# Attention with a router beside it: routing products placed singly and in the seams, division apart from its copy, buffers that run on across blocks

## What is computed

```python
x = layernorm(x + attention(x))            # x: 2 x 2048 x 256, 16 heads of 16
n = layer_norm(x, g1, be1); x = x + n + (n @ mix_w + mix_b)
res = x; n = layer_norm(x, g2, be2)
probs = softmax(n @ router_w); topw, topi = top_k(probs, 2)       # 8 experts
y = sum over the two chosen experts of topw * (silu(n @ w1[e] + b1[e]) @ w2[e] + b2[e])
out = layernorm(x + (res + y))
```

## Time and profile before

| | |
|---|---|
| median of three executions | 1675.38 us |
| the profiled execution | 1675.51 us |
| its span, first to last instruction | 1673.8 us |
| busy: PE, ACT, DVE, POOL | 1610.3, 1244.0, 536.7, 469.3 us |
| exponentials, 116.6 to 1106 | 955.7 us busy of 989 |
| one routed block | 124.17 us |
| mean granted TensorE clock | 0.988 |

### The profile page before, as it was taken

The page is one execution under the profiler, slowest core; times in us unless marked ns, Lnnn a source line. Parts: engine busy times, 40 slices in busy tenths (PEclk is TensorE's granted clock), DMA queues, the critical chain, the costliest instruction groups (busy, mean ns, idle before and its releaser), DMA issues.

```text
span 1673.8 us, 45794 instructions
## 1 busy us (share of the span) xinstructions
PE 1610.3 (96%) x17936; PEld 916.9 (55%) x17941; DVE 536.7 (32%) x1443; ACT 1244.0 (74%) x1869; POOL 469.3 (28%) x495
## 2 busy tenths in 40 slices
PE   7989999999999999999999999999999999999990
PEld 5543333433433433433433433358999999999990
DVE  4551125435435425525525535526210000000004
ACT  5659999999999999999999999963444444444441
POOL 4630011112102202202202212115455444444441
PEclk9999999999999999999999999999999999999995
DMA  5776310101103442301100101646668766666645
GB/s 166 205 155 90 64 40 15 48 26 34 50 24 69 89 81 52 100 28 31 50 28 30 51 26 34 241 143 169 182 175 225 198 185 166 186 186 186 176 119 207
DMA packets 108487, 181.18 MB, mean 108 GB/s; under 512 B 14121, under 2 KB 80361, under 8 KB 108137
## 3 DMA queue, kind: packets, MB, share of 16 engines
q1 hardware_dynamic: 95010, 160.88, 33.2%
q0 software_dynamic: 13296, 17.77, 5.6%
HBM read 134.07 MB, written 40.18 MB: 104 GB/s over the span
## 4 chain that ended last, share of the span: by engine, by line
PE 81%; ACT 4%; issue 4%; DVE 1%; DMA 1%; POOL 0%; POOLq 0%; ACTq 0%; DVEq 0%
PE at_s L1385 24%; PE at_po L1397 23%; PE at_s L1511 14%; PE at_s L1524 14%; ACT place L1300 4%; PE at_small L1413 4%; PE at_small L1406 1%; PE at_po L1500 1%; DMA rows_out<-place,at_v 1%; DVE cb_ln_stats L696 1%; DVE place L1750 0%; POOL place L1254 0%; DMA place<-rows_out 0%; POOL place L1259 0%; DVE at_v L1714 0%
## 5 line engine op out<-in xcount | busy, mean ns | idle before, releaser
L1300 ACT ACTIVATE place<-at_s 128x1024 f32<-128x1024 f32 x1024 | 955.7, 1154 | 34.8 <-PE at_s L1385 33.4
L1385 PE MATMUL at_s<-place 99*32 99x512 bf16 x8192 | 575.3, 381 | 12.7 <-ACT place L1300 7.6
L1397 PE MATMUL at_po<-place,at_v 128*32 128x512 f32 x4096 | 531.7, 594 | 0.0
L1385 PEld LDWEIGHTS at_s<-place 99*32 99x32 bf16 x8192 | 195.0, 95 | 485.6 <-issue 220.2
L1511 PEld LDWEIGHTS at_s<-ex_xT,place 128*128 128x128 f32 x2272 | 264.3, 192 | 5.9 <-issue 1.7
L1317 ACT ACTIVATE place<-at_s,b_turned 128x128 f32<-128x128 f32 x568 | 161.6, 368 | 142.2 <-PE at_s L1511 141.5
L1511 PE MATMUL at_s<-ex_xT,place 128*128 128x128 f32 x2272 | 265.7, 275 | 0.0
L1524 PE MATMUL at_s<-place 128*128 x1136 | 257.0, 379 | 1.1 <-ACT place L1317 0.6
L1524 PEld LDWEIGHTS at_s<-place 128*128 128x128 f32 x1136 | 210.4, 190 | 27.3 <-issue 1.6
L1397 PEld LDWEIGHTS at_po<-place,at_v 128*32 128x32 f32 x4096 | 125.3, 111 | 104.4 <-issue 1.2
L1333 ACT ACTIVATE place<-at_s,at_v 128x256 f32<-128x256 f32 x71 | 33.6, 474 | 162.2 <-PE at_s L1524 156.9
(11 more groups left out here) (216 smaller groups left out, 950.9 us busy)
## 6 DMA issues: line engine op xcount, KB each, us to landing
place<-in_w SPq DMA_DIRECT2D x79, 1024.0 KB, 5.5
place<-k_parts SPq DMA_DIRECT2D x48, 256.0 KB, 5.4
place<-q_parts SPq DMA_DIRECT2D x192, 64.0 KB
at_v<-rows_in SPq DMA_DIRECT2D x71, 129.0 KB, 2.1
place<-in_x SPq DMA_DIRECT2D x8, 512.0 KB, 4.5
at_heads_T<-at_o SPq DMA_DIRECT2D x128, 32.0 KB
rt_x_in<-in_x SPq DMA_DIRECT2D x8, 512.0 KB, 4.1
rows_out<-rt_total SPq DMA_DIRECT2D x8, 512.0 KB, 5.0
```

The costliest lines, as they stand in the source:

```text
L1300: nc.scalar.activation(probs[:, slot(n), :], p_s[n % BUFFERS][:, :], ACT.Exp).then_inc(exp_done, 1)
L1385: last = nc.tensor.matmul(p_s[n % BUFFERS][j:j + 32, s * 512:(s + 1) * 512], k_rows[0:ROWS_M, quad(q).start + h, kt * P + j:kt * P + j + 3 ...
L1397: last = nc.tensor.matmul(p_o[32 * h:32 * h + 32, :], v_one[q % 2][:, h, kt, :], probs[:, slot(q * NG + g), s * 512:(s + 1) * 512], start= ...
```

## The change

The tables of routing jobs change: the output and the mixing product are given one piece at a time, in steps that stand two or four apart, some of them in the seams; turns and the router's product move later. In steps 0 to 2 of a unit the job stands ahead of the weighting round. `copy_out` is cut in two, the copy and `divide`; DVE's order of the two among its other work changes. Score buffers and slots of probabilities count on across blocks, and the experts' buffers follow. The points after the last block change with the tables.

```diff
-    FIRST = (2, 0, 1)
-    OUT_AT = {14: (0, 0), 16: (0, 2), 18: (1, 0), 20: (1, 2)}
-    NORM_AT = {48: 0, 52: 1}
-    MIX_AT = {56: (0, 0), 58: (0, 2), 60: (1, 0), 62: (1, 2)}
-    SENT_AT = {80: 0, 84: 1}
-    ROUTER_AT = {88: 0, 90: 4}
+    OUT_AT = {14: (0, 0), 16: (0, 1), 18: (0, 2), 20: (0, 3), 24: (1, 0), 28: (1, 1), 32: (1, 2), 33: (1, 3)}
+    NORM_AT = {54: 0, 56: 1}
+    MIX_AT = {60: (0, 0), 62: (0, 1), 64: (0, 2), 65: (0, 3), 68: (1, 0), 72: (1, 1), 76: (1, 2), 80: (1, 3)}
+    SENT_AT = {92: 0, 94: 1}
+    ROUTER_AT = {97: 0, 98: 4}
     COUNT_AT = 118
...
+        AFTER = GROUPS * NB
+        p_h = [p_s[(AFTER - 2 + u) % BUFFERS][:, 0:FC * P].rearrange("p (s n) -> p s n", s=FC) for u in range(2)]
+        p_y = [p_s[AFTER % BUFFERS][:, u * 512:u * 512 + D] for u in range(2)]
...
-        TAIL_AT = {2: (14, 16), 3: (18, 20), 9: (48,), 10: (52,), 11: (56, 58), 12: (60, 62),
-                   17: (80,), 18: (84,), 19: (88, 90), 26: (118,)}
+        TAIL_AT = {3: (14, 16, 18, 20), 4: (24, 28, 32, 33), 9: (54,), 10: (56,), 11: (60, 62, 64, 65),
+                   12: (68, 72, 76, 80), 17: (92,), 18: (94,), 19: (97, 98), 26: (118,)}
...
+        def slot(i, n):
+            return (i * NB + n) % RING
+        def scores(i, n):
+            return p_s[(i * NB + n) % BUFFERS]
...
-                        act.wait_ge(scored, i * NB + scored_before(n) + 2 * NG)
-                        act.wait_ge(weighed, i * NR + rounds_reading(held_before(n)) + LEAD)
-                        nc.scalar.activation(probs[:, slot(n), :], p_s[n % BUFFERS][:, :], ACT.Exp
+                        act.wait_ge(scored, i * NB + n + 1 + 2 * NG)
+                        act.wait_ge(weighed, i * NR + rounds_reading(n - RING) + LEAD)
+                        nc.scalar.activation(probs[:, slot(i, n), :], scores(i, n)[:, :], ACT.Exp
...
-                        return product(out_w, heads_T, (2 * half, 2 * half + 1), D, job, (first, first + 1))
+                        return product(out_w, heads_T, (2 * half, 2 * half + 1), D, job, (first,))
...
-                            score(i + 1, FIRST[n + BUFFERS - NB])
+                            score(i + 1, n + BUFFERS - NB)
                         q, g = n // NG, n % NG
+                        if routed and g < 3:
+                            job = job + route(i - 1, n, job)
                         for kt in rounds_at(g):
                             weigh(i, q, kt)
-                        if routed:
+                        if routed and g >= 3:
                             job = job + route(i - 1, n, job)
...
                     v.tensor_copy(o_sb[q % 2][:, :], p_o[:, :]).then_inc(o_copied, 1)
+
+                def divide(i, q):
...
                     add_total(x1, 0)
+                    if beside:
+                        copy_out(i + 1, 0)
                     add_total(x1, 1)
                     dve.wait_ge(small_read, job.first + job.n + 1)
                     layer_norm(v, steps, x1, x1, w)
-                    if beside:
-                        copy_out(i + 1, 0)
                     layer_norm(v, steps, norm1, x1, w)
...
                     turned_half(0)
                     turned_half(1)
+                    if beside:
+                        divide(i + 1, 0)
+                        copy_out(i + 1, 1)
                     dve.wait_ge(total_ready, i * 2 + 2)
                     add_total(x2, 0)
+                    if beside:
+                        divide(i + 1, 1)
                     add_total(x2, 1)
                     dve.wait_ge(small_read, job.first + job.n + 1)
                     dve.sem_inc(x2_ready, 1)
-                    if beside:
-                        copy_out(i + 1, 1)
-                    else:
+                    if not beside:
                         v.tensor_tensor(total[:, :, :], x1[:, :, :], x2[:, :, :], ALU.add).then_inc(kept, 1)
...
                     turned_half(0)
                     turned_half(1)
+                    if beside:
+                        copy_out(i + 1, 2)
                     job.arrived()
...
                     dve.sem_inc(small_read, 1)
                     if beside:
-                        copy_out(i + 1, 2)
+                        divide(i + 1, 2)
...
                     copy_out(i - 1, UNITS - 1)
+                    divide(i - 1, UNITS - 1)
```

More of the change, by code:

```diff
@@ L769, in attend_route_experts @@
     LEAD = 2 * KT
-    FIRST = (2, 0, 1)
     JOBS = 10
-    OUT_AT = {14: (0, 0), 16: (0, 2), 18: (1, 0), 20: (1, 2)}
-    NORM_AT = {48: 0, 52: 1}
-    MIX_AT = {56: (0, 0), 58: (0, 2), 60: (1, 0), 62: (1, 2)}
-    SENT_AT = {80: 0, 84: 1}
-    ROUTER_AT = {88: 0, 90: 4}
+    OUT_AT = {14: (0, 0), 16: (0, 1), 18: (0, 2), 20: (0, 3), 24: (1, 0), 28: (1, 1), 32: (1, 2), 33: (1, 3)}
[3 more added lines that the diff above has]
+    ROUTER_AT = {97: 0, 98: 4}
     COUNT_AT = 118
-    assert NB % RING == 2 and NB % BUFFERS == 2
     with ExitStack() as stack:
@@ L850, in attend_route_experts @@
         rows_now = v_one[0][:, :, :, :].rearrange("p h a w -> p (h a w)")[:, 0:XR * ROW].rearrange("p (r n) -> p r n", r=XR)
-        p_h = [p_s[u][:, 0:FC * P].rearrange("p (s n) -> p s n", s=FC) for u in range(2)]
-        p_y = [p_s[2][:, u * 512:u * 512 + D] for u in range(2)]
+        AFTER = GROUPS * NB
+        p_h = [p_s[(AFTER - 2 + u) % BUFFERS][:, 0:FC * P].rearrange("p (s n) -> p s n", s=FC) for u in range(2)]
+        p_y = [p_s[AFTER % BUFFERS][:, u * 512:u * 512 + D] for u in range(2)]
         p_x = p_o[:, 0:KC * P].rearrange("p (s n) -> p s n", s=KC)
@@ L927, in attend_route_experts @@
         TAIL_TURNS = 3
-        TAIL_AT = {2: (14, 16), 3: (18, 20), 9: (48,), 10: (52,), 11: (56, 58), 12: (60, 62),
-                   17: (80,), 18: (84,), 19: (88, 90), 26: (118,)}
+        TAIL_AT = {3: (14, 16, 18, 20), 4: (24, 28, 32, 33), 9: (54,), 10: (56,), 11: (60, 62, 64, 65),
+                   12: (68, 72, 76, 80), 17: (92,), 18: (94,), 19: (97, 98), 26: (118,)}
         SEND_ROUNDS = {0: (3, 5, 8, 10, 13, 15), 1: (18, 21)}
         ROUTER_AFTER, SEND_AFTER = 10, 15
-        def slot(n):
-            return n % RING if n < NB - 2 else n % RING + 2
-        def held_before(n):
-            earlier = [m for m in range(n) if slot(m) == slot(n)]
-            return earlier[-1] if earlier else max(m for m in range(NB) if slot(m) == slot(n)) - NB
+        def slot(i, n):
+            return (i * NB + n) % RING
+        def scores(i, n):
+            return p_s[(i * NB + n) % BUFFERS]
         def rounds_reading(n):
@@ L1378, in score @@
                     q, g = n // NG, n % NG
-                    if g == 0 or n == 2:
+                    if g == 0:
                         pe.wait_ge(loaded_k[q], (i // QC) * (16 * 6) + 16 * (6 if q == 0 else 7))
@@ L1384, in score @@
                         for j in range(0, P, 32):
-                            last = nc.tensor.matmul(p_s[n % BUFFERS][j:j + 32, s * 512:(s + 1) * 512],
+                            last = nc.tensor.matmul(scores(i, n)[j:j + 32, s * 512:(s + 1) * 512],
                                                     k_rows[0:ROWS_M, quad(q).start + h, kt * P + j:kt * P + j + 32],
@@ L1397, in weigh @@
                         last = nc.tensor.matmul(p_o[32 * h:32 * h + 32, :], v_one[q % 2][:, h, kt, :],
-                                                probs[:, slot(q * NG + g), s * 512:(s + 1) * 512],
+                                                probs[:, slot(i, q * NG + g), s * 512:(s + 1) * 512],
                                                 start=(kt == 0), stop=(kt == KT - 1))
@@ L1442, in route @@
                         half, first = OUT_AT[at]
-                        if first == 0:
+                        if half == first == 0:
                             for u in range(2):
                                 pe.wait_ge(repacked[u], (i + 1) * UNITS * (8 * QUAD))
-                        return product(out_w, heads_T, (2 * half, 2 * half + 1), D, job, (first, first + 1))
+                        return product(out_w, heads_T, (2 * half, 2 * half + 1), D, job, (first,))
                     elif at in NORM_AT:
@@ L1451, in route @@
                         half, first = MIX_AT[at]
-                        return product(mix_w, turned, (2 * half, 2 * half + 1), D, job, (first, first + 1))
+                        return product(mix_w, turned, (2 * half, 2 * half + 1), D, job, (first,))
                     elif at in SENT_AT:
@@ L1547, in _ @@
                 pe.sem_inc(h_ready, 4)
-                for n in FIRST:
+                for n in range(BUFFERS):
                     score(0, n)
@@ L1599, in copy_out @@
                     v.tensor_copy(o_sb[q % 2][:, :], p_o[:, :]).then_inc(o_copied, 1)
+                def divide(i, q):
+                    unit = i * UNITS + q
                     dve.wait_ge(o_copied, unit + 2)
@@ L1720, in _ @@
                     copy_out(0, q)
+                    divide(0, q)
                 dve.wait_ge(loaded_w, 16 * 9)
```

(2 more changed lines are left out.)

2 lines of the change are left out of this document (removed).

## The result

The changed kernel takes 1671.76 us (median of 11, 1668.98 to 1673.53) against 1675.77 for the kernel before beside it (1674.74 to 1676.94, 11 runs): ratio 0.9972, 95% interval 0.9965 to 0.9980. It is 4.0 us faster. The forecast was 7.3 us, 1668.2; the time lies at the upper edge of the range (1671.8), inside it by 0.04 us. The direction was right and the size was little more than half right.

What follows compares the result with a forecast made beforehand. PE and ACT were both taken as nearly full, so PE's order of work counts. Block gains of 9.7 us, less 3.3 for the collision, plus 0.9 after the last block, made 7.3: forecast 1668.2, range 1664.3 to 1671.8.

Steps and rivals of the forecast that it cites:

- The rule of the loop: Timing rule for PE and ACT over a routed block's 128 steps; forecast period 123.25 us instead of 124.17.
- The gaps are single: Sign in ACT's timeline of a routed block: gaps of 0.27 us single rather than in runs of seven.
- The seams: Block starts: next block's first scores written in step 125 instead of 126, removing 0.28 us at each of seven.
- DVE's order: Copy first, division later: work before the turn at 54 needs 18.9 us of 19.3; copies and stores stay in time.
- The collision: Before step 92, POOL's sum of x1 and x2 holds DVE 1.08 us; PE waits 0.47, 3.3 us over seven blocks.
- The chain: DVE's path from the mixing product at step 80 to the turn at 92: 10.18 us, 11.26 with the collision.
- the rival: No collision: small DVE instructions slip between POOL's reads; period 122.8, 10.6 us gained, 1664.9; chance 0.22.
- After the last block: Output products move one point later; an expert's first layer hides PE's 0.86 us wait; 0.86 saved, at worst 0.
- DVE's later division and SP: Division 0 behind the turn of step 56 delays SP's stores and unit 3's query loads to 67; wanted at 93, hidden.
- Only the seams gain: Rival: spreading products only moves waits on a nearly full PE; 2.8 us gained, 1672.7; chance 0.12.
- Slower: Rival: POOL's sum holds DVE's statistics too, PE waits 1.95 us at every step 92; 3.1 slower, 1678.6; chance 0.11.
- four accounts: The forecast (0.55) and three rivals: no collision (0.22), only the seams gain (0.12), slower (0.11).

Runs made afterwards that it cites:

- after: The changed kernel, in its profile taken with the first measurement, against the kernel before: 1671.76 us, ratio 0.9972.
- the kernel with other tables: Changed kernel with quad 1's key loads ahead of the store and POOL's sum later, then pieces, turns and router at other steps: 1670.61 us, ratio 0.9961.

## Why the prediction was right or wrong

**The rule of the loop held.** The forecast period was 123.25 and the blocks took 123.07 to 123.15. The gaps are single, as said, and where the rule puts them; after's block 4 (ACT's timeline):

```profile
633.19 1.94 ACT L1294 ACTIVATE place<-at_s 128x1024 f32<-128x1024 f32 x2 [0.22 <-PE at_s L1379]
635.35 13.55 ACT L1294 ACTIVATE place<-at_s 128x1024 f32<-128x1024 f32 x14 [0.22 <-PE at_s L1379]
```

**The seams** gave 0.29 for the 0.28 predicted; alone they are worth about 2 us, and a kernel with them alone ran at 0.9985.

**DVE's order held.** In after PE has no wait at step 54, none before a product and none at a copy in a seam; the one that its waits view lists for block 4 is 0.3 us, for an exponential. With the division put back, exactly those waits come.

**The collision was real and mis-sized.** DVE's two-input addition was held, the statistics were not. Its term was 1.08 us; it measured 0.97 - 0.17 = 0.80. POOL's sum started 0.14 behind DVE's add (692.38 + 0.69), as worked out. But the statistics started 0.15 behind it, not 0.03, and the small addition ended with the sum instead of taking its 0.17 afterwards. The chain, 11.26 in the prediction, is 0.68 + 0.69 + 0.15 + 8.72 + 0.80 + 0.06 = 11.10, and PE leaves 10.89 where 10.79 was worked out: it should wait 0.21 instead of 0.47. PE's timeline at the turn of step 92 shows 0.76 from the scores to the turn, where 0.54 is the usual distance:

```profile
702.05 0.62 PE L1379 MATMUL at_s<-place 99*32 99x512 bf16 x8
702.81 0.66 PE L1400 MATMUL at_small<-identity,rt_sent_rows 128*128 128x128 f32 x4
```

That is 0.22. The forecast had charged 3.3 us; 7 x 0.22 = 1.5 was due. Of the 0.26 between the two waits the collision was put 0.28 too high and the start of the statistics 0.12 too low, and PE leaves 0.10 more. The period without the collision, 122.8 in the rival, came to 122.9: the rule itself is 0.1 a block too low.

**After the last block** the product stands behind a first layer and has no wait before it, unlike the earlier trace rows; the normalised rows are turned at 1147.36 instead of 1150.12:

```profile
1117.96 3.73 PE L1507 MATMUL at_s<-ex_xT,place 128*128 128x128 f32 x32
1121.62 1.93 PE L1407 MATMUL at_small<-rt_out_w,at_heads_T 128*32 128x256 f32 x32
...
1147.36 0.66 PE L1400 MATMUL at_small<-identity,rt_norm 128*128 128x128 f32 x4
```

From the last exponential to the end were 567.7 us before and 566.9 after, 0.8 less for the 0.86 forecast. The kernel with only the seams, whose points are the old ones, kept 567.7.

**The step that failed** is in the sentence on DVE's later division and SP: "Its four stores on SP's queue, which wait for it, and the query loads of unit 3 behind them, move from about step 61 to 67 ... Hidden", and in what is missing beside it. I followed SP's queue behind the division. I did not follow it behind POOL's sum of x1 and x2. I had the sum moved by 18 steps, asked what it collides with on DVE, and did not ask who waits for it: SP's store, and behind that, once in the whole kernel, key loads. "Hidden" was also the wrong question for a transfer: the data came in time, long before it was wanted. What cost time was when it moved, since loads that had been spread over 13.78 us used the DMA engines without a break. It made 3 to 5 us in one block. The instruction packets and the fall of the clock were in no step of mine, nor was block 0's own bunch of loads, which the kernel before has too. The periods were 0.15 better than forecast, 1 us in all, so the two misses partly hid each other. That the median still lies in the range, by 0.04 us, is luck: the range had no term for this.

**The rivals.** "Only the seams gain" gave 1672.7, and the median is 1671.76, closer than the forecast; yet its reason is refuted, by periods of 123.1 where it says 123.9. "Slower" is refuted by the statistics at 1.41. The time alone would have backed the wrong one of four accounts.

**What is shown and what is not.** "Issue" names no cause, but that PE lacked its program is more than inferred: all 16 stops stand where one packet's 256 instructions end, each before the packet with the same number, and the bunches of loads make and unmake them. The other reading, that the loads disturb PE's reads of SBUF, would have to hit it at these places alone. Not settled is why a packet comes late. Loads that leave as a bunch make it late and the same loads one by one do not, although the DMA engines are as busy; how a packet's turn comes on a DMA engine was not read from the traces. Why it is late by a microsecond more or less from one execution to the next, and with it whether the clock falls, was not tried.

## What to carry to other kernels

When an event is moved, list every engine and queue that waits for it, and for each DMA queue what is issued behind the waiting entry anywhere in the program, also in the one block that differs from the rest. Ask of a moved transfer not only whether the data is in time but which others leave in the same microseconds. And compare the periods of all repeats, not one representative and a total: one block in eight held the whole surprise.

## What was new about the hardware

- The packets of PE's program, 256 instructions each, share the DMA engines with the loads. When six to twelve loads were issued together a packet came up to 17.4 us after the one before, and PE stood still for up to 3.0 us where its instructions ended. It stood whenever it got there less than 2.0 us after the next packet had begun, and nowhere from 2.3 us on. A DMA share near 1.0 is not the sign of it: with the loads one by one it was 1.03 to 1.09 for 30 us, and PE did not stop.
- A pause costs twice when the clock answers it. After 3.02 and 2.5 us without a matmul the granted clock stood at the lower level for most of 4 us, after 2.3 us in another execution it did not; the blocks paid 5.4, 3.8 and 3.1 us. In the kernel with other tables it stayed at 1.00 after a pause of 2.2 us and fell after a second one of 1.9 us, 11 us later (0.77, 0.50 and 0.88 in the three 2 us windows from 574); that block paid 6.6 us. After the single pauses of 0.5 to 1.6 us near 147 us it never fell. So the length of one pause does not tell it.
- A DVE addition of 4 columns (0.17 us) took 0.97 beside a POOL addition of 2.39 us and ended as that did, while the statistics just before it, with one input, kept their 1.41. By the Trainium skill (SBUF — State Buffer, "Who interferes with whom") a DVE instruction with at most one SBUF input, outside the modes that use both of DVE's ports, does not contend with GpSimd, and one with two inputs does with a GpSimd instruction that reads SBUF; this trace agrees with both halves. The same section says that DMA never contends with a compute engine, which speaks against the other reading of the stall.
